# Two token tiles of the shared experts' work, moved from before the sorted tiles of layer 0 to behind them

## The reference

```python
def _L0_ffn_ref(x, router_w, up_w, gate_w, down_w, shared_up_w, shared_gate_w, shared_down_w):
    logits = jnp.einsum('bsd,de->bse', x, router_w)
    probs = jax.nn.softmax(logits, axis=-1)
    topk_vals, topk_idx = jax.lax.top_k(probs, TOP_K)
    top1_val, top1_idx = topk_vals[..., 0], topk_idx[..., 0]
    hid = jnp.einsum('bsd,edh->ebsh', x, up_w) * jax.nn.silu(jnp.einsum('bsd,edh->ebsh', x, gate_w))
    mask = (top1_idx[None, :, :] == jnp.arange(Er)[:, None, None]).astype(x.dtype)
    routed = jnp.einsum('ebsh,ehd,ebs->bsd', hid, down_w, mask)
    shid = jnp.einsum('bsd,dh->bsh', x, shared_up_w) * jax.nn.silu(jnp.einsum('bsd,dh->bsh', x, shared_gate_w))
    shared = jnp.einsum('bsh,hd->bsd', shid, shared_down_w)
    return ALPHA * top1_val[..., None] * routed + shared
```

## Time and profile before

| | |
|---|---|
| Time, median of 3 runs (lowest to highest) | 1564.42 us (1563.73 to 1564.95) |
| Time of the profiled execution | 1563.48 us |
| Its span, first to last instruction | 1561.5 us |
| Instructions | 19860 |
| Mean granted clock of TensorE over the span | 0.952 of full speed |
| Busy: PE / DVE / ACT / POOL | 1331.5 (85%) / 1235.3 (79%) / 967.5 (62%) / 1156.6 (74%) us |
| Shared experts, first to last TensorE instruction (lines 1201 to 1211) | 946.1 to 1064.3 us |
| Sorted tiles, first turn to last down product (lines 1280 to 1302) | 1065.3 to 1178.1 us |
| First instruction of layer 1 on TensorE (line 1567) | 1183.1 us |

### The profile page before, as it was taken

How to read it: one execution, slowest core, us unless ns; L and a number is a source line. 1 busy time by engine, 2 the same in 40 slices (tenths; PEclk the granted TensorE clock), 3 DMA queues, 4 the chain that set the end, 5 groups by cost and what they waited for, 6 DMA issues and landing times.

```text
span 1561.5 us, 19860 instructions
## 1 busy us (share of the span) xinstructions
PE 1331.5 (85%) x6150; PEld 762.7 (49%) x6150; DVE 1235.3 (79%) x1976; ACT 967.5 (62%) x1803; POOL 1156.6 (74%) x684
## 2 busy tenths in 40 slices
PE   6799888988988998898898778398997999986596
PEld 3334334433433443343343234167996666656594
DVE  7899999999999999999999965033335888865375
ACT  6877878777787787877778653024554555441243
POOL 2899999999999999999999983401334566573442
PEclk9899999999999999999999899699998999998798
DMA  5223433333333234333233305301216000020223
GB/s 198 105 90 114 130 125 118 129 103 112 114 130 109 98 128 139 105 126 110 105 119 130 108 27 216 98 1 38 79 52 215 1 2 2 5 64 22 75 67 92
DMA packets 62887, 148.37 MB, mean 95 GB/s; under 512 B 9216, under 2 KB 34304, under 8 KB 53072
## 3 DMA queue, kind: packets, MB, share of 16 engines
q1 hardware_dynamic: 58016, 137.30, 26.0%
q0 software_dynamic: 4768, 9.81, 1.9%
HBM read 134.14 MB, written 18.56 MB: 98 GB/s over the span
## 4 chain that ended last, share of the span: by engine, by line
PE 36%; DVE 24%; issue 13%; ACT 10%; POOL 10%; another core or an unknown queue 4%; DMA 1%; SPq 1%; DVEq 0%; POOLq 0%; ACTq 0%
DVE hh L749 14%; POOL hc L890 7%; PE py L419 4%; DVE hh L734 3%; ACT pa L594 3%; PE pr L1723 2%; PE bank L1292 2%; PE bank L1288 2%; PE bank L1302 2%; PE pr L1924 2%; PE pr L1737 2%; POOL dtu L869 2%; PE bank L1211 2%; PE bank L1201 1%
## 5 line engine op out<-in xcount | busy, mean ns | idle before, releaser
L890 POOL TENSOR_TENSOR hc<-hh,cs 128x1024 f32<-128x1024 f32 x256 | 597.2, 2352 | 4.7 <-DVE hh L749 4.7
L419 PE MATMUL py<-hc,ident 128*128 128x512 f32 x1024 | 486.9, 604 | 5.2 <-POOL hc L890 5.1
L749 DVE TENSOR_TENSOR_SCAN hh<-pa,st,hh 128x512 f32<-128x512 f32 x384 | 466.2, 1264 | 0.5 <-ACT pa L594 0.2
L594 ACT ACTIVATE pa<-dt,w 128x512 f32<-128x512 f32 x512 | 343.6, 684 | 180.9 <-DVE hh L749 179.9
L419 PEld LDWEIGHTS py<-hc,ident 128*128 128x128 f32 x1024 | 197.2, 194 | 228.2 <-issue 208.1
L880 POOL TENSOR_TENSOR hh<-dtu,bs 128x1024 f32<-128x1024 f32 x112 | 262.9, 2348 | 2.8 <-DMA bs<-bcrows 2.8
L734 DVE TENSOR_TENSOR hh<-dtu,pb 128x1024 f32<-128x1024 f32 x144 | 173.1, 1202 | 16.9 <-POOL dtu L869 13.5
L749 DVE TENSOR_TENSOR_SCAN hh<-pa,hh 128x512 f32<-128x512 f32 x128 | 147.9, 1205 | 2.8 <-ACT pa L594 1.9
L1413 POOL DMA_INDIRECT ytoken<-ysort,token x39 | 39.6, 1016 | 141.8 <-ACT ysort L1349 141.2
L331 PE MATMUL pq<-xn,w 128*128 128x512 f32 x248 | 119.1, 605 | 4.1 <-ACT xn L609 2.9
L1768 DVE TENSOR_SCALAR rot<-pr,b 128x128 f32<-128x128 f32 x184 | 51.7, 344 | 47.8 <-remote 26.1
(11 more groups left out here) (319 smaller groups left out, 2533.1 us busy)
## 6 DMA issues: line engine op xcount, KB each, us to landing
cs<-bcrows SPq DMA_DIRECT2D x64, 1024.0 KB, 4.7
bs<-bcrows SPq DMA_DIRECT2D x112, 256.0 KB, 4.3
xsorted<-in_pads SPq DMA_DIRECT2D x13, 387.0 KB, 5.3
rot<-in_rot SPq DMA_DIRECT2D x4, 1024.0 KB, 5.1
wx<-in_l_w SPq DMA_DIRECT2D x4, 1024.0 KB, 9.8
ysort<-ytoken SPq DMA_DIRECT2D x14, 256.0 KB
wx<-in_l_w SPq DMA_DIRECT2D x1, 3072.0 KB, 11.3
wx<-in_l_w SPq DMA_DIRECT2D x1, 2304.0 KB, 16.4
```

The source lines that it names most:

```text
L419: i = pe.matmul(py[:, h * CH:(h + 1) * CH], ident[:, :], hc[s % HCS][:, h, :], start=False, stop=n == NS - 1)
L594: act.activation(pa[i % SLOTS][:, :], dt[m % 2][:, h, :], ACT.Exp, scale=wd[m % 2][:, W_A + h * NS + n:W_A + h * NS + n + 1]).then_inc(s_s ...
L749: v.tensor_tensor_scan(hh[s % HHS][:, h, :], pa[i % SLOTS][:, :], hh[s % HHS][:, h, :], 0.0 if first else st[:, m % 2, n, h:h + 1], ALU.mu ...
L890: g.tensor_tensor(hc[s % HCS][:, :, :], hh[s % HHS][:, :, :], cs[j % 2][:, s % CG, :].unsqueeze(1).broadcast_to([P, HF, CH]), ALU.mult).th ...
```

## The change

The last group of the shared experts (`gg` = 7) does two tiles (256 columns) in place of four. The work for tiles 30 and 31 stands behind the sorted tiles: on TensorE eight up and gate matmuls of 128x256 and 16 down matmuls of 128x128 (`late_rows_tensor`), on ScalarE four Silus of 128x256, on VectorE four products of 128x256 and two sums of 128x128. Since the sorted tiles overwrite `ysort`, and with it `xall`, ScalarE copies the two turned tiles to `late_x` behind its first sorted tile (`late_kept_scalar`). The banks of the late blocks are pairs 0/1, 4/6, 3/5 and again 0/1, so the fourth block waits for VectorE's product of the first. No transfer is added, moved or removed.

```diff
                 NG = NT // 4
+                LATE = 2
+                late_x = ht4[3][:, 0:LATE * P]
+                late_sg = [ht4[2][:, u * LATE * P:(u + 1) * LATE * P] for u in range(2)]
+                late_ht = [ht4[f // 2][:, f % 2 * LATE * P:(f % 2 + 1) * LATE * P] for f in range(FK)]
+                late_up = [b[:, 0:LATE * P] for b in (pt[0], pu[1], pu[0], pt[0])]
+                late_gate = [b[:, 0:LATE * P] for b in (pt[1], pg[1], pg[0], pt[1])]
+
+                def tokens_of(gg):
+                    return 4 - LATE if gg == NG - 1 else 4
+
+                def late_rows_tensor():
+                    pe.wait_ge(s_gxt, NG + 1)
+                    for f in range(FK):
+                        if f in (1, 2):
+                            pe.wait_ge(s_ht, ST + f - 2)
+                        if f == 3:
+                            pe.wait_ge(s_sht, NG * FK + 1)
+                        pe.matmul(late_up[f], ws[:, f * P:(f + 1) * P], late_x, start=True, stop=True)
+                        pe.matmul(late_gate[f], ws[:, FF + f * P:FF + (f + 1) * P], late_x, start=True, stop=True).then_inc(s_sug, 1)
+                    pe.wait_ge(s_ys, ST)
+                    for f in range(FK):
+                        pe.wait_ge(s_sht, NG * FK + f + 1)
+                        for kt in range(LATE):
+                            i = pe.matmul(p_y[kt][:, 0:P], late_ht[f][:, kt * P:(kt + 1) * P],
+                                          ws[:, 2 * FF + f * P:2 * FF + (f + 1) * P], start=f == 0, stop=f == FK - 1)
+                    i.then_inc(s_sdn, 1)
+
+                def late_kept_scalar():
+                    act.wait_ge(s_sdn, NG)
+                    act.activation(late_x, xall[:, (NT - LATE) * P:NT * P], ACT.Identity).then_inc(s_gxt, 1)
+
+                def late_rows_scalar():
+                    for f in range(FK):
+                        act.wait_ge(s_sug, NG * FK + f + 1)
+                        if f >= 2:
+                            act.wait_ge(s_sht, NG * FK + f - 1)
+                        act.activation(late_sg[f % 2], late_gate[f], ACT.Silu).then_inc(s_ssg, 1)
+
+                def late_rows_vector():
+                    for f in range(FK):
+                        v.wait_ge(s_ssg, NG * FK + f + 1)
+                        v.tensor_tensor(late_ht[f], late_up[f], late_sg[f % 2], ALU.mult).then_inc(s_sht, 1)
+                    v.wait_ge(s_sdn, NG + 1)
+                    for kt in range(LATE):
+                        t = NT - LATE + kt
+                        v.tensor_tensor(bx[:, t, :], x1[:, t, :], p_y[kt][:, 0:P], ALU.add).then_inc(s_sadd, 1)
...
-                        cols = slice(gg * 4 * P, (gg + 1) * 4 * P)
-                        pe.matmul(pu[e % 2][:, :], ws[:, f * P:(f + 1) * P], xall[:, cols], start=True, stop=True)
-                        pe.matmul(pg[e % 2][:, :], ws[:, FF + f * P:FF + (f + 1) * P], xall[:, cols], start=True, stop=True).then_inc(s_sug, 1)
+                        n = tokens_of(gg) * P
+                        cols = slice(gg * 4 * P, gg * 4 * P + n)
+                        pe.matmul(pu[e % 2][:, 0:n], ws[:, f * P:(f + 1) * P], xall[:, cols], start=True, stop=True)
+                        pe.matmul(pg[e % 2][:, 0:n], ws[:, FF + f * P:FF + (f + 1) * P], xall[:, cols], start=True, stop=True).then_inc(s_sug, 1)
...
-                    down(NG - 1, (0, 1, 2, 3))
+                    down(NG - 1, range(tokens_of(NG - 1)))
...
                         if j + 4 < ST:
                             turn_xs(j + 4)
+                    late_rows_tensor()
...
                         if j + 4 < ST:
                             kept_up(j + 4)
+                        if j == 0:
+                            late_kept_scalar()
+                    late_rows_scalar()
...
                             kept_gate(j + 4)
+                    late_rows_vector()
```

More of the change, by code:

```diff
@@ L1231, in shared_scalar @@
                             act.wait_ge(s_sht, e - 1)
-                        act.activation(sg[e % 2][:, :], pg[e % 2][:, :], ACT.Silu).then_inc(s_ssg, 1)
+                        n = tokens_of(e // FK) * P
+                        act.activation(sg[e % 2][:, 0:n], pg[e % 2][:, 0:n], ACT.Silu).then_inc(s_ssg, 1)
                 def shared_vector():
@@ L1236, in added @@
                         v.wait_ge(s_sdn, gg + 1)
-                        v.tensor_tensor(bx[:, gg * 4:gg * 4 + 4, :], x1[:, gg * 4:gg * 4 + 4, :], view(p_sh[gg % 2], 4, P),
+                        n = tokens_of(gg)
+                        v.tensor_tensor(bx[:, gg * 4:gg * 4 + n, :], x1[:, gg * 4:gg * 4 + n, :], view(p_sh[gg % 2], n, P),
                                         ALU.add).then_inc(s_sadd, 1)
@@ L1243, in hidden @@
                             v.wait_ge(s_sdn, (e - 6) // FK + 1)
-                        v.tensor_tensor(ht4[e % 6][:, :], pu[e % 2][:, :], sg[e % 2][:, :], ALU.mult).then_inc(s_sht, 1)
+                        n = tokens_of(e // FK) * P
+                        v.tensor_tensor(ht4[e % 6][:, 0:n], pu[e % 2][:, 0:n], sg[e % 2][:, 0:n], ALU.mult).then_inc(s_sht, 1)
                     choose_vector()
```

2 lines of the change are left out of this document (1 added, 1 removed).

## The result

The changed kernel takes 1558.22 us (median of 7 executions, 1555.33 to 1563.84); the kernel before takes 1564.42, timed beside it (7 executions, 1563.73 to 1569.04). The ratio of the two is 0.996, with a 95% interval of 0.9946 to 0.9974; ratios further down are given in the same way, against the kernel before. The profiled execution of after has a span of 1556.3 us and a time of 1558.22: 5.2 less than the span of before. The change did what it says and the time went the way forecast, but 2 us further in the medians and 1 us further in the spans.

What follows compares the result with a forecast made beforehand. TensorE was taken to bound the kernel up to the end of the sorted tiles, then SyncE at the phase end. -5.1 + 0 + 0.9 + 0 = -4.2 us from the 1564.42 median gave 1560.2, range 1558.4 to 1563.2.

Steps and rivals of the forecast that it cites:

- Front, -5.1: Layer 0's last shared group, ahead of the sorted tiles: halved work takes out 1.7 + 1.3 + 1.8 + 0.3 = 5.1 us.
- Block 28: First block of the last shared group: instructions 0.85 us shorter, nothing gained, as block 29 waits for VectorE's product of block 27.
- Copy, 0: ScalarE's added 128x256 copy behind its first sorted tile: taken as 0, at most 0.6 us once.
- Tail, +0.9: Behind the sorted tiles: late work outlasts TensorE's 4.96 us idle, so layer 1 starts at 1184.0, not 1183.1; 0.9 us lost.
- the rival of serial blocks: Late blocks run one after the other, losing 3.3 us in place of 0.9: 1562.6 us, chance 0.07.
- Clock at layer 1's start, 0: TensorE's clock still falls after the late work, only later; taken as 0 us.
- The rival in which the late work keeps the clock up: Full clock through layer 1's first chunk, 0.7 and 0.2 us more gained: 1559.3 us, chance 0.13.
- 1.2 GHz in the late work: TensorE granted half clock there, 5.25 us become 10.5, net +1.0: 1565.4 us, chance 0.06.
- a low clock over the dense part: Layer 1's first dense matmuls run at half clock, up to 3.5 us more: about 1562.2 us, chance 0.15.
- from the second chunk on layer 1 looks as before: Sign expected in the profile: layer 1 unchanged from its second chunk on, only 4.2 us earlier.
- The mechanism's sum, -4.2: Whole kernel: front -5.1, copy 0, tail +0.9 and clock 0 add to -4.2 us.
- theory B: Raised after the first measurement: the change shifts layer 1 against something and so shortens it whenever run, some 2 us.

Runs made afterwards that it cites:

- after_fill: The changed kernel with 20 identity matmuls of 128x128 added where TensorE waits in layer 1's last retention chunk: 1496.75 us, ratio 0.9962 against the kernel before.
- after_fill2: The changed kernel with the same 20 added matmuls, timed again beside a slower kernel before (1565.52 us): 1557.33 us, ratio 0.9951.
- clears_later: The changed kernel with VectorE's four clears at layer 1's start moved behind its first rotation: 1500.34 us, ratio 0.9977 against the kernel before.
- filled base: The kernel before with 20 identity matmuls added in layer 1's last retention chunk: 1499.72 us, ratio 0.9981; timed again 1560.93 us, ratio 0.9977.
- first group: Kernels timed together: the kernel before (1564.42 us) and the changed kernel (1558.22 us).
- fourth group: Kernels timed together: both filled kernels again, filled without late work, and filled with clears moved; the kernel before took 1565.52 us.
- second group: Kernels timed together: both kernels repeated unchanged, and the change's two halves, one each; the kernel before took 1500.86 us.
- after_again: The changed kernel run again, unchanged: 1498.28 us, ratio 0.9987 against the kernel before.
- the third: Kernels timed together: two filled kernels, the changed kernel with clears moved, and one moving three tiles; the kernel before took 1502.79 us.
- front_only: The changed kernel without the late work, so tiles 30 and 31 get no shared experts: 1497.9 us, ratio 0.9985 against the kernel before.
- tail_only: The changed kernel with all four tiles in the last shared group and the late work done a second time: 1504.1 us, ratio 1.003 against before.
- before_again: The kernel before run again, unchanged: 1501.4 us, ratio 1.0005 against the kernel before.

## Why the prediction was right, and where it was wrong

- **Front, -5.1: right.** Measured 5.1 to 5.2 from block 27's product to the first turned tile, in all four pairs of profiles. Its parts hold too: blocks 29 and 30 gave 1.6, block 31's chain 1.96 as worked out and so 1.3, the down products and VectorE's sum 2.05. Block 28 gave 0.14 and not nothing: TensorE's own matmuls had no gap before block 29 in before (1050.18 follows 1049.32 by the usual 0.86 for two); only the weight load had. The idle time before block 29's load grew to 0.95 and not to 1.4, since block 28's last load starts behind only two of the four shortened instructions (2 x 0.21).
- **Copy, 0, and sorted tiles: right.** 112.8 us in all profiles.
- **Tail, +0.9: right in after, too small where the returns land late.** 0.95 in after, and no wait for a bank, so the rival of serial blocks is out. Two small errors cancel there: VectorE's two sums took 0.48 and not 0.56, and layer 1 opened 0.11 (TensorE) to 0.20 (VectorE) behind them and not 0.06. In 3 of the 8 profiles that have late work (after_fill, after_fill2, clears_later) the last return landed 1.6 to 2.1 us later (3.9 to 4.4 us in place of 2.2 or 2.3), and in none of the 6 without. Then SyncE ends the wait, and in the two of them that can be measured the tail costs 1.6 and 2.1. Whether the late work causes that or it is chance in 14 profiles stays open.
- **Clock at layer 1's start, 0: right.** The fall came later, as said, and the chunk behind it lost 0.5 us that the second chunk took back (the first score product comes 13.4 us after layer 1's start in place of 12.9, the first sum of its outputs 35.5 in place of 35.6). The rival in which the late work keeps the clock up is out: it still falls, 1184.3 against 1182.9. So are the rivals of 1.2 GHz in the late work (1.00 there) and of a low clock over the dense part (it is back 2 us earlier). The busy share that the prediction read for the sparse part, 4.69 of 10 us, is of a window with idle and dense work in it; from 1183.08 to 1188.78 TensorE is busy 3.47 of 5.70 us.
- **The failed step** is the bound on the clock: "from the second chunk on layer 1 looks as before", with 0 for it and a range built from layer 1's start alone. The earlier trace rows show one fall; the trace of before has seven more in layer 1, among them one in the middle of the retention (1339.9 to 1343.3) and the two in the last chunk, 1391 to 1398 and 1405 to 1411.6, at 0.51 and 0.50. The prediction priced none of them. Those in the last chunk are worth 4 us or more of retention (first to last reciprocal 216.1 to 217.3 where it was low for 14 to 20 us, 211.6 to 211.9 where for 3.4 us or not at all, all of these with the fall in the middle; without that fall 211.5 at 6.8 us, and 209.2 to 210.6 at 3.4 us or none), with either kernel, and pull the time down or up by as much as the whole forecast. In the first pair of profiles that is what the runs showed in place of the 0: the retention is 3.9 us shorter in after, with 3.4 us of low clock in the last chunk against 13.7, and 1.8 us of it come back behind. The mechanism's sum, -4.2, was good for -3.0 to -3.7 by time on the filled base.
- **What a measurement can tell from no change was set too fine.** The three executions of before that the prediction knew lie within 1.2 us, and it took 3.1 us for what can be told from no change; the clusters are 5 to 7 us apart. All seven of before's executions in the first group (1563.7 or more) fit the upper cluster that the fourth group shows for this kernel, and five of the seven of after (1555.3 to 1559.1) lie near its lower cluster less the forecast 4.2 us (1555.5 to 1557.1). That split is the likely source of the part of the 6.2 beyond -4.2; each kernel has one profile in this group, so it is not shown execution by execution.

Not tested is a weaker form of theory B: that the change, by shifting layer 1, alters how often the clock falls in the last chunk. The split of seven in seven against two in seven has a chance of about 0.02 if the odds were the same. In the second group there is no sign of it (7 of 47 executions of before at a mean clock of 0.965 or less, 4 of 12 of after_again), but the odds differ between groups for one kernel (14 of 31 in the third), and the changed kernel without filler was not timed again where before takes 1565 us.

The Trainium skill ("TensorE: Matmul & The Clock Gate", Part 1: The HAM clock gate) says that the number of matmuls that run slow differs between runs of one kernel, and counsels not to fit it. The two profiles of the changed kernel, 211.8 and 217.3 us, agree. The page puts the penalty of that ramp below 1% of a typical span; here the clusters lie 7 us apart in 1500, so that holds as well, but a change of 0.3% is smaller than it.

Open: why front_only and tail_only, timed on the unfilled base, came out 2 us away from their stages each. The clock in the last chunk does not explain it, since the distance is the same inside the cluster of the higher clock. The fall in the middle, 1.5 us, and late landings are candidates; only one execution of each has a profile.

## What to carry to other kernels

Ask the trace for every stretch with a low granted clock before the range is set, not only for those beside the change: a thin stretch where it can fall is a lottery that each execution draws again. When a change is worth less than that lottery, first fill the thin stretch, in the kernel before and in the changed one, and compare those; the stages read from two profiles are the cheaper measure, as long as the clock's falls in both are set side by side. Work moved under a wait is free only for as long as the wait lasts: count from TensorE's own last start, and stop at the tile that sticks out.

## What the chip showed

**Filler pays by itself.** Twenty useless matmuls made the kernel before 0.2% faster (0.9981 and 0.9977, both intervals below 1), and the granted clock in the last chunk was 1.00 in every filled profile.

**One program, 63 us apart.** The same kernel takes 1564 to 1566 us in the first and the fourth group and 1501 to 1503 in the second and the third. A slower chip is not shown as the cause: the second group ran on chip number 14, and both the third and the fourth on number 13; for the first no number is known. Windows of before, then of before_again, over the scatters at the end of layer 0's Mamba part and over the first returns of layer 1:

```profile
965.00:998.00 33.00, 13.19 (x57) 7.50 (x55) 3.36 (x5) 1.79 (x3) 25.07 (x27) 0.75 0.16 53
1455.00:1490.00 35.00, 28.68 (x230) 28.50 (x231) 19.13 (x73) 12.19 (x30) 14.66 (x16) 0.84 0.13 41
```

```profile
967.00:999.00 32.00, 32.00 (x147) 20.02 (x146) 10.73 (x16) 7.16 (x12) 24.28 (x26) 1.00 0.17 53
1428.00:1460.00 32.00, 32.00 (x289) 32.00 (x288) 23.11 (x90) 13.21 (x33) 24.22 (x26) 1.00 0.32 99
```

GpSimd issues its 32 scatters at the same pace (39.4 us from first to last in both), but in the first windows VectorE does 5 instructions in place of 16 and TensorE 57 in place of 147. When the stall ends in before, ScalarE has waited for nothing that the profile shows, and VectorE for something outside the core's known queues:

```profile
999.98 0.60 ACT L1232 ACTIVATE xt<-bank 128x512 f32<-128x512 f32 x1 [28.12 <-issue]
...
1003.68 1.31 DVE L1244 TENSOR_TENSOR xt<-bank,xt 128x512 f32<-128x512 f32 x2 [31.09 <-remote]
```

It ends just after the last scatter (997.80). The front is 67.5 us in before and 38.3 in before_again, and the 46 returns of layer 1 take 92.8 and 64.5 from first to last: together 57.6, where the medians differ by 63.0 and the spans of the two profiles by 55.4. That both stand beside indirect transfers is shown; what differs between the groups is not.
